# A three-product split of the output projection in a fused attention and cell kernel, and its place among the other products

## The reference, cut to what matters

```python
Q, K = (x @ Wq.T), (x @ Wk.T)              # 16 heads of 64
V = x @ Wv.T                               # 16 heads of 16
dl, dt = x @ Wdl.T, softplus(x @ Wdt.T + dt_bias)
...                                        # decay and level factors from dl and dt
Wmat = scores * decay * lam_ts             # causal, per head
Y = einsum('bhts,bshd->bthd', Wmat, V).reshape(B, T, 256)
o = Y @ Wout.T + x                         # the output projection
o = layernorm(o) * ln_g + ln_b
x = layernorm(x + o)
...                                        # the gated cell on x, and a last layernorm
```

## Time and profile before

| | value |
|---|---|
| median of 3 runs | 690.88 us (690.83 to 691.87) |
| the profiled execution | 691.23 us |
| its span, first to last instruction | 689.4 us |
| PE busy | 667.5 us, 97% of the span |
| weight loads busy | 604.7 us, 88% |
| DVE, ACT, POOL busy | 473.2, 339.6, 348.2 us |
| mean granted clock of PE | 0.981 |

### The profile page before, as it was taken

One profiled execution on the slowest core, in us unless ns is written; L12 is line 12 of the kernel. 1 busy time (PEld: TensorE's weight loads), 2 busy tenths in 40 slices (PEclk: granted clock), 3 DMA queues, 4 the chain that ended last, 5 costly groups with the idle time before them and its releaser, 6 DMA issues.

```text
span 689.4 us, 22147 instructions
## 1 busy us (share of the span) xinstructions
PE 667.5 (97%) x9194; PEld 604.7 (88%) x9194; DVE 473.2 (69%) x1072; ACT 339.6 (49%) x759; POOL 348.2 (51%) x471
## 2 busy tenths in 40 slices
PE   9799999999999999999999999999978999999994
PEld 7699999999999999899999999999967888888894
DVE  3854877769786868667696868688896435454546
ACT  5545454445545554444455455545433434555555
POOL 2705555646465565656364655655455125343434
PEclk9999999999999999999999999999987899999998
DMA  8112130303131221203031212213032000000002
GB/s 303 40 45 58 41 88 11 98 7 94 30 70 41 60 57 42 68 2 98 8 91 32 68 48 52 69 31 82 3 98 63 1 1 1 31 31 31 31 32 92
DMA packets 53588, 37.09 MB, mean 54 GB/s; under 512 B 5360, under 2 KB 52080, under 8 KB 53488
## 3 DMA queue, kind: packets, MB, share of 16 engines
q1 hardware_dynamic: 53488, 35.67, 19.0%
HBM read 30.41 MB, written 5.24 MB: 52 GB/s over the span
## 4 chain that ended last, share of the span: by engine, by line
PE 90%; DVE 3%; ACT 2%; SPq 1%; DMA 1%; POOL 1%; issue 1%; POOLq 0%; DVEq 0%; ACTq 0%
PE bank L383 66%; PE bank L386 6%; PE bank L407 5%; PE bank L474 5%; PE bank L439 5%; PE bank L503 4%; SPq L330 1%; DMA xt<-in_wffn 1%; DVE t L982 1%; ACT t L751 0%; DVE st L1279 0%; DVE hh L979 0%; DMA scr<-cT 0%; DVE t L979 0%; ACT QT L751 0%
## 5 line engine op out<-in xcount | busy, mean ns | idle before, releaser
L383 PE MATMUL bank<-xH,wH 128*128 128x256 f32 x480 | 144.6, 301 | 0.0
L383 PE MATMUL bank<-xL,wH 128*128 128x256 f32 x480 | 135.0, 281 | 0.0
L383 PE MATMUL bank<-xH,wL 128*128 128x256 f32 x480 | 134.3, 280 | 0.0
L979 DVE TENSOR_TENSOR W<-bank,E 128x512 f32<-128x512 f32 x128 | 82.2, 684 | 34.7 <-PE bank L383 34.7
L383 PEld LDWEIGHTS bank<-xH,wH 128*128 128x128 f32 x480 | 90.5, 189 | 6.3 <-issue 5.5
L383 PEld LDWEIGHTS bank<-xL,wH 128*128 128x128 f32 x480 | 90.7, 189 | 0.4
L383 PEld LDWEIGHTS bank<-xH,wL 128*128 128x128 f32 x480 | 90.5, 188 | 0.0
L751 ACT ACTIVATE E<-bank 128x512 f32<-128x512 f32 x128 | 66.1, 603 | 49.0 <-PE bank L407 49.0
L751 ACT ACTIVATE QT<-bank 128x512 f32<-128x512 f32 x64 | 38.2, 596 | 100.7 <-PE bank L383 100.7
L383 PE MATMUL bank<-QT,KT 64*128 64x128 f32 x1024 | 65.9, 278 | 1.2 <-ACT E L751 1.2
L383 PEld LDWEIGHTS bank<-QT,KT 64*128 64x128 f32 x1024 | 59.7, 188 | 5.6 <-ACT E L751 1.5
(11 more groups left out here) (151 smaller groups left out, 1686.9 us busy)
## 6 DMA issues: line engine op xcount, KB each, us to landing
cB<-scr SPq DMA_DIRECT2D x240, 64.0 KB, 2.9
xt<-in_xT SPq DMA_DIRECT2D x16, 256.0 KB, 3.0
xs<-in_x SPq DMA_DIRECT2D x16, 256.0 KB, 3.2
out<-xs SPq DMA_DIRECT2D x16, 256.0 KB, 2.1
xt<-in_wffn SPq DMA_DIRECT2D x8, 256.0 KB, 3.1
QT<-in_wqk SPq DMA_DIRECT2D x4, 256.0 KB, 5.8
KT<-in_wqk SPq DMA_DIRECT2D x4, 256.0 KB, 6.1
scr<-cT SPq DMA_DIRECT2D x16, 64.0 KB, 1.9
```

The lines of the kernel that those rows point to most:

```text
L383: return e.matmul(o, a, b, start=start, stop=stop)
L979: return e.tensor_tensor(o, a, b, op)
```

## The change

The output projection takes the split form. The weights of Wout land in a tile that is free early (`zt`), ACT makes their high part in step 1 and POOL their low part. `turn_y` writes to `zs`; a new `split_y` of ACT, at the head of step n = 1, copies it to `ytH`; a new `split_y` of DVE makes `ytL` behind the first quarter of W (k = 0 of u = 0). PE's `out_proj` now has six products: four with `ytH`, for which it waits on ACT (`a_yt`), and, behind a wait on DVE (`d_yl`), two with `ytL`. `decays` moves one step later and behind `project`: from between `out_proj` and `project` of step n = 2 to between `project` and `state` of step n = 3; DVE's copy to `cgt` moves with it, behind DVE's `state`. The tile `x1` goes, its values stand in `xs`.

```diff
@@ token_jobs
-    for d, j in ((12, 7), (0, 0), (0, 1), (1, 2), (3, 8), (5, 3), (7, 4), (8, 5)):
+    for d, j in ((12, 7), (0, 0), (0, 1), (1, 2), (3, 8), (6, 3), (7, 4), (8, 5)):
@@ misc_jobs
-        if s % 4 == 3 and cc < CB - 1:
-            out += [("state", ci, 0)]
     for sg, j in token_jobs(s):
         if j == 3:
             out += [("cgt", sg, 0)]
+    if 0 <= s < NG and s % 4 == 3 and cc < CB - 1:
+        out += [("state", ci, 0)]
...
@@ PE, out_proj
-                e.wait_ge(d_yt, ci + 1)
+
+                e.wait_ge(a_yt, ci + 1)
                 if ci == 0:
-                    e.wait_ge(l_wo, 16)
-                for k in range(2):
-                    t = mm(YB[:, 256:512], yt[:, 128 * k:128 * k + 128], wo[:, k, :], k == 0, k == 1)
+                    e.wait_ge(g_wo, 1)
+                for k in range(2):
+                    c = slice(128 * k, 128 * k + 128)
+                    mm(YB[:, 256:512], ytH[:, c], woH[:, k, :], k == 0, False)
+                    mm(YB[:, 256:512], ytH[:, c], woL[:, k, :], False, False)
+                e.wait_ge(d_yl, ci + 1)
+                for k in range(2):
+                    c = slice(128 * k, 128 * k + 128)
+                    t = mm(YB[:, 256:512], ytL[:, c], woH[:, k, :], False, k == 1)
                 t.then_inc(p_op, 1)
@@ PE, the order in a step
                 if (c1 := chunk_at(s, 6)) is not None:
                     out_proj(c1)
+                for sg, j in project_jobs(s):
+                    project(sg, j)
                 for sg, j in token_jobs(s):
                     if j == 3:
                         decays(sg)
-                for sg, j in project_jobs(s):
-                    project(sg, j)
                 if n == 3 and ci in STATE:
                     state(ci)
@@ ACT
+            def split_wo():
+                e.wait_ge(l_wo, 16)
+                act(woH[:, :, :], wo0, ACT.Copy).then_inc(a_wo, 1)
+
+            def split_y(ci):
+                e.wait_ge(d_yt, ci + 1)
+                if ci:
+                    e.wait_ge(p_op, ci)
+                act(ytH[:, :], zs[ci % 2][:, :], ACT.Copy).then_inc(a_yt, 1)
...
                 if 0 <= s < NG and s % 4 == 0:
                     exps(s // 4)
+                if (ci := chunk_at(s, 5)) is not None:
+                    split_y(ci)
                 if (sg := split_x_at(s)) is not None:
                     split_x(sg)
+                if s == 1:
+                    split_wo()
@@ DVE
                     tt(W[:, hs, :], XP[2 * u + k][:, :].rearrange("p (h t) -> p h t", h=4), E[:, hs, :],
                        ALU.mult).then_inc(d_w, 1)
+                    if u == 0 and k == 0 and ci:
+
+                        split_y(ci - 1)
...
+            def split_y(ci):
+                e.wait_ge(a_yt, ci + 1)
                 if ci:
                     e.wait_ge(p_op, ci)
...
+                tt(ytL[:, :], zs[ci % 2][:, :], ytH[:, :], ALU.subtract).then_inc(d_yl, 1)
...
+                if s == NG + 1:
+                    split_y(NC - 1)
@@ POOL
+                if s == 1:
+                    e.wait_ge(a_wo, 1)
+                    tt(woL[:, :, :], wo0, woH[:, :, :], ALU.subtract).then_inc(g_wo, 1)
...
-                    tt(x1[:, :], oo[:, :], xs[:, ci, :], ALU.add).then_inc(g_x1, 1)
+                    tt(xs[:, ci, :], oo[:, :], xs[:, ci, :], ALU.add).then_inc(g_x1, 1)
```

More of the change, by code:

```diff
@@ L88, in misc_jobs @@
             out += [("cgt", sg, 0)]
+    if 0 <= s < NG and s % 4 == 3 and cc < CB - 1:
+        out += [("state", ci, 0)]
+    for sg, j in token_jobs(s):
         if j == 5:
@@ L173, in program @@
         xt = [sb(f"xt{i}", [P, 2, 256]) for i in range(2)]
-        wo = sb("wo", [P, 2, 256])
+        woH, woL = [sb(n, [P, 2, 256], F32R) for n in ("woH", "woL")]
         cs = sb("cs", [P, C_CT])
@@ L177, in program @@
         fvs = sb("fvs", [P, 8])
-        yt = sb("yt", [P, 256])
+        ytH, ytL = [sb(n, [P, 256], F32R) for n in ("ytH", "ytL")]
         oo = sb("oo", [P, 256])
-        x1 = sb("x1", [P, 256])
         st1 = sb("st1", [P, 6])
@@ L252, in program @@
         wt0 = W[:, :, :].rearrange("p h t -> p (h t)")[:, 0:928].rearrange("p (k n) -> p k n", k=2)
+        wo0 = zt[:, 0:2, :]
         w0 = [t[:, :, :].rearrange("p m t -> p (m t)") for t in (QT[1], KT[1])]
@@ L271, in program @@
         p_in, p_st, p_op, p_cf = sem("p_in"), sem("p_st"), sem("p_op"), sem("p_cf")
+        g_wo = sem("g_wo")
         g_v0, g_s0 = sem("g_v0"), sem("g_s0")
@@ L277, in program @@
         a_dv, a_dec, a_coef = sem("a_dv"), sem("a_dec"), sem("a_coef")
-        a_e = sem("a_e")
+        a_e, a_wo, a_yt = sem("a_e"), sem("a_wo"), sem("a_yt")
         a_wf, a_c0, a_yh, a_g = sem("a_wf"), sem("a_c0"), sem("a_yh"), sem("a_g")
@@ L285, in program @@
         d_red, d_ct = sem("d_red"), sem("d_ct")
-        d_w, d_yt, d_S = sem("d_w"), sem("d_yt"), sem("d_S")
+        d_w, d_yt, d_yl, d_S = sem("d_w"), sem("d_yt"), sem("d_yl"), sem("d_S")
         d_oo, d_mv1, d_nn, d_mv2, d_x2 = [sem(n) for n in ("d_oo", "d_mv1", "d_nn", "d_mv2", "d_x2")]
@@ L343, in _ @@
             e.dma_start(C[:, :, :].rearrange("p h l -> p (h l)"), cst[:, C_CT:C_END]).then_inc(l_c, 16)
-            e.dma_start(wo[:, :, :], kt(wout)).then_inc(l_wo, 16)
+            e.dma_start(wo0, kt(wout)).then_inc(l_wo, 16)
             load_x(0)
@@ L1051, in turn_y @@
             def turn_y(ci):
+                z = zs[ci % 2][:, :]
                 e.wait_ge(p_y, 2 * ci + 2)
+                if ci in INTER:
+                    e.wait_ge(d_own, summed[ci])
+                    tt(z, YB[:, 0:256], z, ALU.add).then_inc(d_yt, 1)
+                else:
+                    if ci >= 2:
+                        e.wait_ge(a_yt, ci - 1)
+                    e.tensor_copy(z, YB[:, 0:256]).then_inc(d_yt, 1)
+            def split_y(ci):
+                e.wait_ge(a_yt, ci + 1)
                 if ci:
                     e.wait_ge(p_op, ci)
[L1056 to L1060, removed]
+                tt(ytL[:, :], zs[ci % 2][:, :], ytH[:, :], ALU.subtract).then_inc(d_yl, 1)
             def state(ci):
@@ L1128, in outer_stats @@
                 e.wait_ge(g_x1, ci + 1)
-                e.bn_stats(st2[:, :], x1[:, :]).then_inc(d_own, 1)
+                e.bn_stats(st2[:, :], xs[:, ci, :]).then_inc(d_own, 1)
                 made += 1
@@ L1135, in outer_norm @@
                 e.wait_ge(g_rs2, ci + 1)
-                e.tensor_scalar(xs[:, ci, :], x1[:, :], mv2[:, 0:1], rs2[:, 0:1], ALU.subtract, ALU.mult).then_inc(d_x2, 1)
+                e.tensor_scalar(xs[:, ci, :], xs[:, ci, :], mv2[:, 0:1], rs2[:, 0:1], ALU.subtract, ALU.mult).then_inc(d_x2, 1)
             def tokens(sg, j):
```

## The result

The changed kernel takes 695.14 us (median of 9 runs, 693.62 to 698.51), the kernel before 690.88 (9 runs, 690.21 to 691.87). The ratio is 1.0063 with a 95% interval of 1.0048 to 1.0078, so it is slower by 3.3 to 5.4 us. The forecast was 692.1 us with a range up to 694.2: the sign held, the size did not.

The account below looks back on a forecast made before the run. PE was taken as the bound up to chunk 28 and from chunk 31's gates on; -2.3 + 2.2 + 0.9 + 0.45 = +1.25, taken as +1.2, gave 692.1 us against a median of 690.88, range 690.2 to 694.2.

Parts of the forecast that it names:

- The products: PE's output projection: six split products take 0.71 for 0.86, saving 0.15 at each of 15 chunks, 2.3 us.
- the bubble: Odd chunks 1 to 27: second project waits 0.31 for the bank 0 copy, 1.14 between loads; 0.16 lost each, 2.2 us.
- step 2: Early step without a projection: moved decays no longer hides behind the bank 0 copy, adding its whole 0.90 us.
- The rival that PE doesn't wait for the copy: Odd chunks: the 14 bubbles of 0.31 on PE fall away, giving 687.8 us, faster; chance 8%.
- the shorter pitch: Rival at the projection: products paced at 0.107 instead of 0.118 save 1.0 us more, giving 691.1; chance 5%.
- DVE 32 subtractions at 0.42 (like its addition into `yt`): DVE's added work for ytL: 32 subtractions of 128x256, each priced at 0.42 us.
- The room on DVE: DVE's queue behind the subtraction: at odd chunks 1.4 us of room before the transpose is needed, so no loss taken.
- the one with the least room: Chunk 15, with no inter: ytH comes just in time, inside the bubble anyway; no loss taken.
- DVE becomes the bound: Rival behind even chunks: the added 0.42 delays exponents by 0.25 in 14 places, 3.5 us, giving 695.6; chance 13%.
- 0.45 lost: Chunk 31, among the cell's products: ACT's split_y delays the gates and c1L, so a PE load starts 0.45 us later.
- The prediction's +1.2: Whole kernel: the net of all terms, +1.25 us, taken as +1.2 us slower.
- its rival of the clock: Between 515 and 539 us: stretches at 1.2 GHz fall otherwise, up to 2 us either side; chance 12%.

Follow-up runs that it names:

- e6: The change with y left in its bank, read there by ACT's copy and DVE's subtraction, PE waiting for ytL ahead of all six products: 695.31 us, ratio 1.0060.
- e12: The change with y left in its bank and 6 zero products of 512 columns at the start for 11 of 256: 693.01 us, ratio 1.0028.
- e9: The change with y in its bank, chunk 31's ytH on DVE, decays back behind the six products, 6 zero products of 512 columns at the start: 687.88 us.
- e5: The change with 1 zero product at the start where it has 11: 694.35 us, ratio 1.0062.
- e8: The change with y in its bank, 1 zero product at the start, decays between high and low products, chunk 31's ytH on DVE: 688.86 us, ratio 0.9976.
- e11: The kernel before with only its zero products changed, for 60 more weight loads at the start: 696.73 us, ratio 1.0105.
- e4: The change with ytL made for chunk 0 only, so 31 subtractions fewer on DVE and an incomplete result: 695.03 us, ratio 1.0062.
- e7: The change with the ytL subtraction of chunks 0 to 30 on POOL, ahead of levels, instead of DVE: 694.49 us, ratio 1.0058.
- e1: The change measured again unaltered, with a profile of another execution, against the kernel before: 696.39 us, ratio 1.0079.
- e10: As e9, but with the 11 zero products of 256 columns back at the start: 688.64 us, ratio 0.9957.

## Why the prediction was wrong, and where it was right

**The products, the bubble, step 2: right to 0.02 us each.** 0.71 per projection, 1.16 for 1.14 between the loads, +0.16 and -0.15 in turn, +0.9 in B. The rival that PE doesn't wait for the copy is out, and so is the shorter pitch: 155.00 to 155.71 for six is 0.118 each.

**The failed step: "DVE 32 subtractions at 0.42 (like its addition into `yt`)".** They took 0.93 in the mean, 1.30 at odd chunks and 0.53 at even ones. The row chosen as the nearest was near in size, 128x256, and not in what it touches: the addition reads a bank, the subtraction only SBUF. The kernel before had the better row, also of 128x256:

```profile
136.03 1.08 DVE L979 TENSOR_TENSOR zs<-zt 128x256 f32<-128x256 f32 x1
```

while POOL ran

```profile
135.55 1.27 POOL L1351 TENSOR_TENSOR prod<-ll,cs 128x512 f32<-128x512 f32 x1
```

By it the subtraction had to be priced at 0.4 to 1.1, with the high end at odd chunks, where `levels` runs. In the change this sum comes later, when POOL does nothing, and takes 0.43:

```profile
138.16 0.43 DVE L1002 TENSOR_TENSOR zs<-zt 128x256 f32<-128x256 f32 x1
```

The Trainium skill, "SBUF — State Buffer", section "Who interferes with whom", says that a DVE instruction with two SBUF inputs contends with a GpSimd instruction that reads SBUF, and one with at most one SBUF input (and no 2-port mode) doesn't. e6 agrees: 0.41 for 1.30. The same page of the Trainium skill names `copy` among the operations that can enter a 2-port mode and then contend; `C<-ll` at 1.25 beside `xL` agrees.

**The room on DVE: "Behind an odd chunk ... 1.4 of room for 0.42".** At chunk 5 the room held even for 1.30. It was read at one chunk and taken for all. Behind chunk 13's subtraction stands a longer sum of `inter` (`zt` of 384 columns and one more addition), and there 1.2 plus the 1.1 of the delayed copy were too much. The third wait, at chunk 15, is for the subtraction itself; the prediction had named this chunk as the one with the least room, and looked there at `ytH` alone. The rival "DVE becomes the bound" had the right engine, and put it at the even chunks, 14 times 0.25; it came in three places, with 1.6 in all. Of D's +1.8, e6 takes 1.5 away again.

**Not foreseen at all: the stop in G, 1.7 us.** The prediction costed the added products at their pitch and didn't ask what the two more weight loads per chunk do to the length of PE's program. The profile of the kernel before gives no hint of it, since there load 8357 (536.09) is the third of a row of `W`,`V` products, right behind idle times of 1.02 and 0.33, and no stop stands at it.

**The end: "0.45 lost".** The step came as told:

```profile
549.17 0.42 ACT L760 ACTIVATE ytH<-zs 128x256 fp32r<-128x256 f32 x1 [0.62 <-DVE zs L1002]
549.49 1.83 ACT L760 ACTIVATE g<-bank,b 128x512 f32<-128x512 f32 x3
...
554.92 0.19 PEld L385 LDWEIGHTS bank<-c1H,wH 128*128 128x128 f32 x1 [0.37 <-POOL c1L L1386]
```

This is a wait of 0.37 for `c1L`. Its effect is lost in the scatter of I.

**The sum.** The prediction's +1.2, plus 1.6 for D (1.8, less the 0.2 it had there), plus 1.7 for G gives +4.5; the medians gave +4.3. That they agree to 0.2 is partly luck: the sections of the change's two profiles sum to +2.5 and +4.6, as A, F, H and I fall differently, and whether these sections average to those of the kernel before isn't shown. e12 looks from the other side: with the long subtraction gone and the stop out of G, +2.0 is left where +1.2 was forecast. Of the remaining 0.8, D still has 0.2, and the stop that moved to H would by its length be 0.9 more; no run is without it and else the same. The 0.8 is also within the intervals (e12's reaches from 0.8 to 3.2).

## What to carry to other kernels

Price an added vector operation by a row of the same place, not only of the same size: ask whether its operands are in SBUF or in a bank and what the engine beside it runs at that moment, and read the room behind it at the fullest iteration, not at the first. If one operand can stay in its bank, that may cost nothing and shield it. And when a change makes an unrolled program longer, compare where stops with no releaser stand before and after, before explaining the difference by the change's own work.

## What the runs showed of the hardware

**PE's program arrives in pieces, and a piece can come late.** There is a stop of 0.9 to 2.0 us at weight load 8357, which edits at the very start moved (e9, e12), removed (e5, e8) and provoked (e11). The delivery is seen too: from the end of an instruction packet to the end of the stop it is 1.24 to 1.47 us in all nine. Where there is no stop, PE came to this load later than that or at the lower edge of it: 1.32 behind the packet's end in e8, 2.24 in e5 and 2.57 in e4, which has the change's number of loads, and where PE ran at 0.50 behind a wait of 3.44. What starts a packet, and why this one comes late, stays open.

**The granted clock makes the scatter of section H.** The 36 products of the first bias take 3.9 us in e5 and e7, and 6.4 in e1, whose windows are

```profile
522.80:529.00 6.20, 4.72 (x162) 4.09 (x163) 2.74 (x4) 3.46 (x8) 2.49 (x4) 1.00 0.29 86
529.40:536.20 6.80, 6.80 (x40) 6.80 (x38) 4.54 (x11) 0.63 (x1) 3.90 (x6) 0.59 0.01 2
```

(stretch, sum, busy by engine, granted clock, DMA share, GB/s), and e5's

```profile
530.00:534.10 4.10, 4.10 (x40) 4.10 (x38) 3.93 (x9) 0.63 (x1) 1.28 (x3) 1.00 0.19 61
```

The same 38 loads take 6.8 at a clock of 0.59 and 4.1 at 1.00. The waits for `CT` and `E` and the stop lie ahead of it: e1, e6 and e11 have all three, and 6.3 to 6.4 us for the 36. But e10 has all three too and 5.8, and the first profile of the change and e7 have the stop and 4.2 and 3.9; so none of these alone decides it, and what does stays open. (e12 takes 6.3 besides its stop, which lies within the 36.) This is the loss that the prediction gave as its rival of the clock, up to 2 us either side; it was 2.5.
